# Another split of a rounding step between ScalarE and VectorE: 768 and 1280 columns in place of 1024 and 1024

## The reference

```
def _affine_quantize(x):
    amin, amax = (jnp.min(x), jnp.max(x))
    scale = jnp.maximum((amax - amin) / 255.0, 1e-08)
    zp = jnp.clip(jnp.round(-amin / scale) + QMIN, QMIN, QMAX)
    q = jnp.clip(jnp.round(x / scale) + zp, QMIN, QMAX)
    return (q, scale, zp)

def _qlinear(x, W, b):
    xq, sx, zx = _affine_quantize(x)
    wq, sw = _sym_quantize(W)
    acc = jnp.einsum('bsh,oh->bso', xq - zx, wq)
    return acc * (sx * sw) + b

h = _qlinear(x, W1, b1)                  # 128 features to 512
h = jax.nn.gelu(h, approximate=False)
out = _qlinear(h, W2, b2)                # 512 to 128
```

## Time and profile before

| | us |
|---|---|
| median of 3 runs | 2460.99 |
| lowest and highest run | 2459.72, 2462.21 |
| profiled execution, its own time | 2461.15 |
| profiled execution, its span | 2459.3 |
| TensorE, VectorE, ScalarE busy | 2272.6, 1853.0, 1497.2 |

### The profile page before, as it was taken

One profiled execution on the slowest core, in us unless ns is written; L12 is line 12 of the kernel. 1 busy time (PEld: TensorE's weight loads), 2 busy tenths in 40 slices (PEclk: granted clock), 3 DMA queues, 4 the chain that ended last, 5 costly groups with the idle time before them and its releaser, 6 DMA issues.

```text
span 2459.3 us, 49180 instructions
## 1 busy us (share of the span) xinstructions
PE 2272.6 (92%) x14859; PEld 1954.4 (79%) x14861; DVE 1853.0 (75%) x4361; ACT 1497.2 (61%) x3089; POOL 523.5 (21%) x734
## 2 busy tenths in 40 slices
PE   7899999999899899995478999999997999979998
PEld 6788888888789788883157888888886887879998
DVE  3688787787966788887984877888888666866666
ACT  5555655656444677776896666666663654636665
POOL 2032221322211212121001111111102442422333
PEclk9999999999999999998559999999998999989999
DMA  8444544445300444440015455555442000115445
GB/s 213 113 127 118 146 130 126 130 118 144 101 16 0 124 130 131 133 123 27 0 36 147 135 142 149 145 137 143 130 138 62 1 1 4 35 52 140 136 135 153
DMA packets 461643, 256.56 MB, mean 104 GB/s; under 512 B 25664, under 2 KB 442332, under 8 KB 461532
## 3 DMA queue, kind: packets, MB, share of 16 engines
q1 hardware_dynamic: 461532, 255.27, 37.5%
HBM read 150.10 MB, written 105.12 MB: 104 GB/s over the span
## 4 chain that ended last, share of the span: by engine, by line
PE 74%; DVE 12%; ACT 6%; issue 5%; DVEq 1%; POOL 0%; ACTq 0%; DMA 0%; POOLq 0%
PE ps_o L905 12%; PE ps_s L889 11%; PE ps_p L87 7%; PE ps_p L89 6%; PE ps_p L88 6%; PE ps_t L878 6%; PE ps_o L1393 3%; PE ps_t L1393 2%; DVE a_e L1164 2%; PE ps_s L87 2%; DVE a_sm L1156 2%; PE ps_t L3023 2%; PE ps_s L88 2%; PE ps_o L3023 2%; ACT a_keys L1017 2%
## 5 line engine op out<-in xcount | busy, mean ns | idle before, releaser
L905 PEld LDWEIGHTS ps_o<-a_val,a_pt 128*128 128x128 f32 (+2 forms) x3200 | 415.3, 193 | 34.8 <-issue 9.1
L889 PE MATMUL ps_s<-a_keys,a_zt 128*128 128x308 f32 (+1 forms) x1024 | 418.3, 493 | 17.5 <-ACT a_keys L1017 9.8
L905 PE MATMUL ps_o<-a_val,a_pt 128*128 128x128 f32 (+2 forms) x3200 | 425.9, 277 | 6.8 <-ACT a_pt L1054 4.0
L1156 DVE TENSOR_REDUCE a_sm<-a_e 128x16 f32<-128x1232 f32 (+1 forms) x192 | 234.5, 1221 | 229.0 <-ACT a_e L1062 228.9
L1026 ACT ACTIVATE a_stage<-ps_p 128x512 f32<-128x512 f32 (+1 forms) x370 | 220.9, 597 | 287.7 <-PE ps_p L89 285.4
L1054 ACT ACTIVATE a_pt<-ps_t 128x512 f32<-128x512 f32 (+1 forms) x448 | 225.3, 505 | 162.0 <-PE ps_t L878 161.7
L1017 ACT ACTIVATE a_keys<-ps_p 128x308 f32<-128x308 f32 x603 | 257.2, 427 | 101.3 <-PE ps_p L89 100.8
L1145 DVE TENSOR_REDUCE a_mx<-ps_s 128x6 f32<-128x462 f32 (+1 forms) x512 | 255.9, 550 | 49.2 <-PE ps_s L889 29.2
L878 PE MATMUL ps_t<-ident,a_e 128*128 128x128 f32 (+1 forms) x1600 | 262.7, 277 | 31.1 <-DVE a_e L1164 28.9
L87 PE MATMUL ps_p<-ct_hi,a_mt_hi 96*128 (+1 forms) x603 | 259.3, 430 | 0.0
L1148 DVE TENSOR_TENSOR a_e<-ps_s,a_mx 128x462 f32<-128x462 f32 (+1 forms) x512 | 254.3, 548 | 0.0
(11 more groups left out here) (433 smaller groups left out, 4653.4 us busy)
## 6 DMA issues: line engine op xcount, KB each, us to landing
a_vals<-a_stage SPq DMA_DIRECT2D x160, 512.0 KB, 3.5
a_val<-a_vals SPq DMA_DIRECT2D x128, 576.0 KB
f_w<-in_L_ffn_W_dram SPq DMA_DIRECT2D x129, 256.0 KB, 2.7
a_vals<-a_stage SPq DMA_DIRECT2D x40, 416.0 KB
a_val<-a_vals SPq DMA_DIRECT2D x64, 256.0 KB
a_val<-a_vals SPq DMA_DIRECT2D x128, 40.0 KB
x<-in_x_dram SPq DMA_DIRECT2D x8, 512.0 KB, 7.2
out_dram<-x SPq DMA_DIRECT2D x7, 512.0 KB, 5.7
```

Source lines behind the costliest of these rows:

```text
L889: mm = eng.matmul(o, zt, keys[:, h0:h0 + nh, :], start=True, stop=not self.masked)
L905: mm = eng.matmul(c.ps_o[:, (i % 2) * P:(i % 2 + 1) * P], self.pt[0:r, n, :], self.val[0:r, i % 2, n, :], start=(n == 0), stop=(n == self. ...
L1156: eng.tensor_reduce(self.sm[:, :], e, AX.X, ALU.add).then_inc(st.sem, 1)
```

## The change

`integers` is split at column 768 in place of column 1024, in all groups but the first. Group 0 goes on in halves, since its two places are two separate tiles. Both engines write the same 2048-column place as before, and TensorE reads it as before; numbers and order of instructions, waits and semaphores are the same on every engine.

```diff
+    CUT = 768
...
+    def share(self, g, par, first, mine):
+        if first:
+            half = 0 if mine == "scalar" else 1
+            return (self.h[:, ds(g, 1), 2 * half:2 * half + 2, :].rearrange("p a c t -> p (a c t)"),
+                    self.hq(g, par, True, half))
+        cols = slice(0, self.CUT) if mine == "scalar" else slice(self.CUT, self.F * GT)
+        units = self.h[:, ds(g, 1), :, :].rearrange("p a c t -> p (a c t)")
+        place = self.h[:, 0, 2 * par:2 * par + 2, :].rearrange("p c t -> p (c t)").bitcast(BF16)
+        return units[:, cols], place[:, cols]
...
 VectorE:
         def integers(g, par, first=False):
-            h = self.h[:, ds(g, 1), 2:4, :].rearrange("p a c t -> p (a c t)")
+            units, place = self.share(g, par, first, "vector")
...
-            eng.tensor_scalar(self.hq(g, par, first, 1), h, self.sc[:, 1, 6:7], None, ALU.add)\
+            eng.tensor_scalar(place, units, self.sc[:, 1, 6:7], None, ALU.add)\
                .then_inc(self.high_ready.sem, 1)
...
 ScalarE:
         def integers(g, par, first=False):
-            h = self.h[:, ds(g, 1), 0:2, :].rearrange("p a c t -> p (a c t)")
+            units, place = self.share(g, par, first, "scalar")
...
-            eng.activation(self.hq(g, par, first, 0), h, ACT.Identity, bias=self.sc[:, 1, 6:7])\
+            eng.activation(place, units, ACT.Identity, bias=self.sc[:, 1, 6:7])\
                .then_inc(self.low_ready.sem, 1)
```

## The result

The changed kernel takes 2456.48 us (median of 20 runs, 2454.46 to 2460.34), the kernel before, run beside it, 2462.44 us (20 runs, 2459.62 to 2465.78). The ratio is 0.9978, with a 95% interval of 0.9971 to 0.9985: about 5.4 us less, between 3.7 and 7.1 (the difference of the two medians is 5.96). The forecast was 3.0 us less, 2458.0 us, with a range of 2456.3 to 2460.0. The measured median lies inside the range, at its lower edge; the gain is nearer to twice the forecast than to it.

What follows compares the result with a forecast made beforehand. ScalarE, busy without a gap, was taken to bound the part. Fourteen savings of 0.213 us, 2.98 us in all, were to bring the median from 2460.99 to 2458.0 us, range 2456.3 to 2460.0.

Steps and rivals of the forecast that it cites:

- ScalarE bounds the part, and its instruction gets 0.213 us shorter: In the part's loop, ScalarE sets the pace; 256 fewer columns at 0.834 ns bring steps from 3.03 to 2.81 us.
- the other slope: For ScalarE's integers, 0.93 ns a column from integers at 1024 against shift at 2048 columns: 0.237 us less per group.
- VectorE stays hidden with 0.13 us to spare: In each step, VectorE's integers grow 0.131 us to about 877 ns, within its 0.48 us of idle time.
- The slower rival: VectorE becomes the bound if 1280 columns run at 1.11 ns each: 1.6 us slower, 2462.6 us; chance 0.03.
- Fourteen savings of 0.213 us: ScalarE's integers of groups 1 to 14 each save 0.213 us on the path: 2.98 us.
- The clock stays low in the part: TensorE's clock stays at 0.50 through the part; the rival, a rise inside it, gave 1.1 us more, 2456.9; chance 0.08.
- the equality of the clock over all eleven steps: Argument against a clock rise: in mid-part TensorE stayed at 0.50 over eleven steps while 77% busy.
- the fourteenth saving: At the part's end, the integers of group 14 start the last output but one: another 0.213 us.
- The low stretch behind the part: Rival: the next phase's low-clock stretch, 1.7 us, falls away or comes twice: 2456.3 or 2459.7; chance 0.10.
- The sum: Over the part, 14 x 0.213 = 2.98 us less, arriving whole in the total; ends 2.1 and 3.3 us.
- the case that I gave 0.72: Main case for the whole kernel: ScalarE's saving arrives without a clock gain, 2457.0 to 2459.3 us; chance 0.72.
- Faster by over 0.2%: Verdict for the whole kernel, below 2456.1 us: needs the saving and a clock gain together; chance 0.05.

Runs made afterwards that it cites:

- kernel 4: The changed kernel without the bias matmul, so the output bias is missing from the result; ratio to the kernel before 0.9988, part 48.70 us.
- kernel 3: The kernel before, in halves of 1024, with each group's bias matmul issued twice; ratio to the kernel before 0.9993, part 50.57 us.
- kernel 1: The kernel before run again without an edit, beside the kernel before; ratio 0.9994 (0.9985 to 1.0003), part 51.87 us.
- kernel 8: The changed kernel with each group's bias matmul issued twice; ratio to the kernel before 0.9969, part 47.93 us.

## Why the prediction was right or wrong, point by point

- *ScalarE bounds the part, and its instruction gets 0.213 us shorter*: right. 920 ns against 1133, steps of 2.81 us. The slope taken from one form at two sizes was the right one; the other slope would have said 2.79. From the figures of the Trainium skill ("ScalarE: Activation LUTs", What ACT_TABLE_LOAD costs) the estimate for 768 columns with one such operand is 919 ns, and the trace agrees with 920.
- *VectorE stays hidden with 0.13 us to spare*: right, 879 ns and 0.13 us, though the sum left out the overlap with the next instruction, so that the slack is 0.21. The slower rival is out: the slope of 0.512 ns a column held up to 1536 columns (1.01 us).
- *Fourteen savings of 0.213 us*: right. The first piece is 2.99 us shorter in all three profiles of the change, and in kernel 4 as well, where the clock is low throughout.
- *The clock stays low in the part (its rise was the rival at 0.08)*: this is the step that failed. I let "the equality of the clock over all eleven steps" speak against a rise, but those eleven steps were one and the same load; they said nothing of a load with 0.49 us idle in place of 0.71. The clock rose in the part in all three profiles of the change, and in every other kernel with more TensorE work per time than before, and stayed at 0.50 in the three of before and in kernel 4, with less. That it follows from how densely TensorE works is shown from both sides, by kernel 3 and kernel 4; whether the share of busy time counts or the length of a single gap, no run separates. Its price was put at 1.1 us and measured at 0.94. The difference is an error of the sum: with the high clock VectorE's integers of 15 release the last output, so the fourteenth saving is no longer on the path, and the 1.1 us counted it again. 1279.6 - 0.21 - 1278.5 = 0.9 us was right, and with it the forecast would have been 2457.1, not 2456.9.
- *The low stretch behind the part (rival at 0.10)*: it does occur, and is larger than I priced it: at the next phase's start alone there are 0, 3.4 or 6.8 us of low clock (1.00, 0.83 and 0.66 in windows of 10 us), and the pieces behind the part differ by up to 5.5 us (1177.7 to 1183.2) where I had allowed 1.7 to either side. The three profiles of before alone differ by 3.4.
- *The sum*: the part gave 3.93 us, of which 2.98 are the forecast's, and the three measured ratios of the change say 5.4, 3.9 and 6.4 us. The part's 3.93 us are a ratio of 0.9984, which all three intervals hold, the third at its very end. Weighted by their widths the three give about 0.9979, between 0.9974 and 0.9984 (an estimate), so that the part alone stands at the edge. The 1 to 2 us beyond it belong to no instruction of the part, and the kernel before against itself has shown as much (0.9994 in kernel 1). By the cuts, I hold low stretches behind the part for their cause, but the pieces behind it in the three profiles of the change (1182.5, 1182.4, 1179.3 us) are no shorter than those of before (1179.7, 1179.6, 1183.0), so for this kernel it is argued and not shown.
- *The range, 2456.3 to 2460.0*: 2456.48 lies in it partly by luck. The forecast starts from 2460.99, the median of three runs; the 20 runs have 2462.44, 1.45 us more. From 2460.99 the measured ratio leads to 2455.6, below the range, and the case that I gave 0.72, with the clock low, did not occur.
- *Faster by over 0.2%: 0.05*: too little. It treated the clock's rise as an accident apart from the saving, where the saving itself brings it about.

## What to carry to other kernels

Where an engine works in a fixed rhythm, its slack and the slopes of its instructions give the gain of a moved share to 0.01 us a step; compare one form at two sizes, since operands have a price of their own. When a step gets shorter, every other engine gets denser: ask what TensorE's clock does at the new density, and not only which engine is late. And a gain of a few us is best read from the stretch that was changed, in several profiles, since what lies behind can move by as much.

## What the runs showed that I had not expected

**The clock can rise under a load with gaps.** With 0.50 us idle in each 2.81, TensorE went to full speed in the part, and there it needs only half the time, so that it is idle for more than half; it then fell back and rose again. In kernels 3 and 8, with one more matmul of 512 columns per group, it stayed high (0.97 and 0.98 in the mean). The Trainium skill ("TensorE: Matmul & The Clock Gate", A second HAM failure mode: psum-queue depth-cycling) tells of a kernel whose clock goes back and forth as TensorE idles briefly and often between groups of matmuls. The trace agrees, with gaps of 0.5 us at the low level and ScalarE as what TensorE waits for.

**Useless matmuls can shorten a part.** Kernel 3 does 16 more matmuls than before and its part is 1.29 us shorter, all of it behind the last output but one. A gain of the whole is not shown (0.9993, 0.9984 to 1.0003), and with the new split the same edit leaves the part as it is (kernel 8).

**The clock's changes keep step with the work.** In the three profiles of the changed kernel ScalarE's first shift starts at 1225.80, 1225.89 and 1224.13 us, and the first rise in the part comes 11.9, 11.8 and 11.5 us behind it. The changed kernel first, then its third profile:

```profile
1237.00:1238.00 1.00, 0.90 (x12) 0.91 (x13) 1.00 (x2) 1.00 (x2) 0.00 (x0) 0.65 0.00 0
```

```profile
1235.00:1236.00 1.00, 0.57 (x9) 0.58 (x10) 1.00 (x2) 1.00 (x2) 0.00 (x0) 0.66 0.00 0
```

(A mean of 0.65 over the window is 0.30 us at the high level, so the rise is at 1237.70; likewise 1235.68.) So work arrives at the part at nearly the same place relative to the clock's changes, though the times up to it differ by up to 4.7 us between the 14 profiles (1.8 between these three). This would explain why the length of a part decides which low stretches come behind it, the same way more often than not, and why the cut at 896 gains 7.4 and 7.9 us with a part only 2.0 us shorter. Its two profiles have 1178.0 and 1177.9 us behind the part, some 1.7 us below the shorter and 5.0 below the longest of before. But the three profiles of the changed kernel agree for some 600 us behind L922 and not further on, and no run here moves the work without changing the part; it stays open. The fastest kernels of the study by their runs are the cut at 896 and the change with two bias matmuls, and by the part the cut at 640; the intervals of all of them overlap.
